# Second context attention: the order of three evacuations, and the context padded to 128 rows

## The reference

```
qh = (LN(x) @ Wq + bq)    16 heads of 8 channels
kh = ctx @ Wk + bk        77 x 128, from ctx of 77 x 64
vh = ctx @ Wv + bv
attn = softmax(qh kh^T / sqrt(8)) over the 77 context rows
x = x + concat(attn vh) @ Wo + bo
```

## Time and profile before

| | before |
|---|---|
| median of 3 runs | 4045.31 us |
| the profiled execution | 4050.56 us |
| its span | 4048.8 us |
| PE / PEld busy | 3845.5 us (95%) / 3012.5 us (74%) |
| DVE / ACT / POOL busy | 2922.8 (72%) / 2792.6 (69%) / 1902.7 us (47%) |
| granted TensorE clock, mean | 0.983 |
| the sublayer of the change | 3278.6 to 3689.2 us of the span |

### The profile page before, as it was taken

The page is one execution under the profiler, slowest core; times in us unless marked ns, Lnnn a source line. Parts: engine busy times, 40 slices in busy tenths (PEclk is TensorE's granted clock), DMA queues, the critical chain, the costliest instruction groups (busy, mean ns, idle before and its releaser), DMA issues. The chain is left out here.

```text
span 4048.8 us, 109312 instructions
## 1 busy us (share of the span) xinstructions
PE 3845.5 (95%) x35786; PEld 3012.5 (74%) x35786; DVE 2922.8 (72%) x7397; ACT 2792.6 (69%) x6292; POOL 1902.7 (47%) x1726
## 2 busy tenths in 40 slices
PE   8999899999989999898999989999999989998999
PEld 6777687888756666675666677888888867776777
DVE  7888655555479999658999955776777767775665
ACT  5555455555579999747999965777777767774333
POOL 5555322222278888526777753333333321112444
PEclk9999899999989999999999999999999989999999
DMA  1000100000100000100000010000000000000000
GB/s 30 19 19 19 52 7 6 6 6 6 41 9 8 8 8 8 29 16 9 8 8 8 12 29 30 1 0 0 0 0 0 0 3 3 3 3 6 12 12 13
DMA packets 118477, 46.71 MB, mean 12 GB/s; under 512 B 92256, under 2 KB 117088, under 8 KB 117728
## 3 DMA queue, kind: packets, MB, share of 16 engines
q1 hardware_dynamic: 118368, 45.30, 4.3%
HBM read 24.36 MB, written 4.19 MB: 7 GB/s over the span
## 5 line engine op out<-in xcount | busy, mean ns | idle before, releaser
L1102 POOL TENSOR_TENSOR l_rc<-l_rc,l_rs 128x1024 f32<-128x1024 f32 x128 | 303.7, 2373 | 202.3 <-DVE l_rs L1294 193.0
L1169 ACT ACTIVATE l_prob<-l_prob,l_mx 128x128 f32<-128x128 f32 x1024 | 312.9, 393 | 0.0
L670 POOL TENSOR_TENSOR ca_prob<-ca_prob,ca_sm 128x1232 f32<-128x1232 f32 x64 | 144.0, 2250 | 299.3 <-DVE ca_sm L836 299.3
L1780 POOL TENSOR_TENSOR mb_steps<-w_upto,mb_dta 128x1024 f32<-128x1024 f32 x64 | 121.5, 1898 | 345.7 <-DVE mb_dta L2048 345.7
L1194 PE MATMUL l_qk_ps<-w_local,l_hT 128*128 128x512 f32 x512 | 249.1, 610 | 13.0 <-DVE l_rs L1294 11.2
L1096 POOL TENSOR_TENSOR l_prob<-l_prob,l_sm 128x1024 f32<-128x1024 f32 x128 | 243.0, 1898 | 20.5 <-DVE l_sm L1280 20.5
L1079 POOL TENSOR_TENSOR l_rc<-l_rc,l_ss 128x1024 f32<-128x1024 f32 x128 | 243.6, 1903 | 12.5 <-POOL l_rc L1102 4.5
L1939 PE MATMUL mb_x_ps<-w_wx,mb_xT 128*128 128x256 f32 x1024 | 237.2, 385 | 0.0
L382 ACT ACTIVATE la_ef<-la_feat,la_fbias 128x1024 f32<-128x1024 f32 x128 | 135.7, 1111 | 121.8 <-PE la_feat L441 121.8
L2507 POOL TENSOR_TENSOR mo_hid<-mo_hid,mo_gate 128x1024 f32<-128x1024 f32 x64 | 121.8, 1903 | 201.3 <-DVE mo_hid L2653 201.3
L346 POOL TENSOR_SCALAR la_ef<-la_ef,la_high,la_low 128x1024 f32<-128x1024 f32 x128 | 151.4, 1193 | 134.6 <-ACT la_ef L382 134.6
(11 more groups left out here) (349 smaller groups left out, 11860.7 us busy)
## 6 DMA issues: line engine op xcount, KB each, us to landing
la_xin<-in_x SPq DMA_DIRECT2D x64, 64.0 KB
la_xT<-in_x_T SPq DMA_DIRECT2D x64, 64.0 KB, 1.8
l_h<-lt_y SPq DMA_DIRECT2D x128, 32.0 KB
lt_quad<-lt_y SPq DMA_DIRECT2D x32, 128.0 KB
out_x<-k_x SPq DMA_DIRECT2D x64, 64.0 KB, 1.5
l_h<-lt_y SPq DMA_DIRECT2D x128, 31.8 KB
lt_quad<-lt_y SPq DMA_DIRECT2D x32, 127.0 KB
ca_ctxT<-in_ctx_T SPq DMA_DIRECT2D x128, 19.2 KB
```

The source lines that it names most:

```text
L1102: gp.tensor_tensor(wide(rc[l][:]), wide(rc[l][:]), wide(rs[l][:]), ALU.add).then_inc(*pool_sum.did("rot"))
L1169: ex = sc.activation(p[:, a, j], p[:, a, j], ACT.Exp, bias=mx[l][:, a, j:j + 1])
```

## The change

On VectorE the value evacuation moves behind the reciprocal and the product. On ScalarE the keys are evacuated ahead of the queries; the waits that meant "both done" now name the queries, and the scores on TensorE wait for the queries too. `ctxT` gets 128 rows, of which the lower 64 are cleared once; `wk` and `wv` are taken with all 128 rows, so that the key and value products run over 128 rows. At the start GpSimd clears the small buffers and `ctxT` first and `vpad` last; the other engines no longer wait for `vpad`, only the value evacuation of the unrolled steps does. The transfers of the context wait for the clearing of `ctxT` once.

```diff
--- before.py
+++ after.py
@@ -2126,13 +2126,13 @@
     with ExitStack() as stack:
         m = Memory(nc, stack, "xa")
         part = g.context_part
-        wq, wk, wv, wo = part["wq"], part["wk"][0:CD], part["wv"][0:CD], part["wo"]
+        wq, wk, wv, wo = part["wq"], part["wk"], part["wv"], part["wo"]
         bq, bk, bv, bo = part["bq"], part["bk"], part["bv"], part["bo"]
         hmask, gmask = m.sb("hmask", [C, H]), m.sb("gmask", [C, 4])
         eps = m.sb("eps", [128, 1])
         stats, mv, rstd = both(m, "stats", [T, 6]), both(m, "mv", [T, 2]), both(m, "rstd", [T, 2])
         xn, xnT, qT = both(m, "xn", [T, C]), both(m, "xnT", [C, T]), both(m, "qT", [C, T])
-        ctxT, kT = both(m, "ctxT", [CD, S]), both(m, "kT", [C, S])
+        ctxT, kT = both(m, "ctxT", [128, S]), both(m, "kT", [C, S])
         kblock = both(m, "kblock", [C, 4, S])
         vpad = [m.sb(f"vpad{i}", [128, H // 2, 2 * WIDE]) for i in range(4)]
         prob = [m.sb(f"prob{i}", [T, H, S]) for i in range(4)]
@@ -2145,6 +2145,7 @@
         qkv_ps = m.ps("qkv_ps", [128, 512])
         out_ps = m.ps("out_ps", [128, 512])
         zeroed, prep, scaled, made = (m.sem(n) for n in ("zeroed", "prep", "scaled", "made"))
+        padded, cleared = m.sem("padded"), m.sem("cleared")
         c_in = m.lanes("c_in")
 
         vec_norm = Stage(m.sem("vec_norm"), "stats mv xn")
@@ -2153,7 +2154,7 @@
         vec_out = Stage(m.sem("vec_out"), "rden att attT x")
         act_norm = Stage(m.sem("act_norm"), "lnv rstd")
         act_turn = Stage(m.sem("act_turn"), "xnT")
-        act_key = Stage(m.sem("act_key"), "qT kT")
+        act_key = Stage(m.sem("act_key"), "kT qT")
         act_soft = Stage(m.sem("act_soft"), "exp")
         act_prob = Stage(m.sem("act_prob"), "pT0 pT1")
         act_out = Stage(m.sem("act_out"), "oT")
@@ -2164,7 +2165,7 @@
         pool_norm = Stage(m.sem("pool_norm"), "xb")
         pool_key = Stage(m.sem("pool_key"), "kb")
         NORM, TURN, KEY, SOFT, PROB, OUT = 0, 1, 2, 3, 5, 6
-        NZERO = 6
+        NZERO, NCLEAR = 2, 8
         by_head = lambda ap: ap.rearrange("p j (k e) -> p j k e", k=2)
         one = lambda b: flat(g.x[:, bass.ds(b.index, 1), :])
 
@@ -2177,24 +2178,28 @@
                         index = b.index if b.trip is None else sp.snap(b.index)
                         src = d["ctx_T"][bass.ds(index, 1)].rearrange("b c s -> (b c) s")
                         sp.wait_ge(*pe_key.at("qkv", b, ago=2))
-                        sp.dma_start(ctxT[b.lane][:], src).then_inc(c_in[b.lane], 16)
-
+                        sp.dma_start(ctxT[b.lane][0:CD], src).then_inc(c_in[b.lane], 16)
+
+                sp.wait_ge(padded, 2)
                 pipeline(sp, g.NB, OUT + 2, step, turn=4)
 
             @block.gpsimd
             def _(gp):
-                for i in range(4):
-                    gp.memset(vpad[i][:], 0.0).then_inc(zeroed, 1)
                 gp.memset(eps[:], LN_EPS).then_inc(zeroed, 1)
                 gp.memset(hmask[:], 1.0).then_inc(zeroed, 1)
+                for l in (0, 1):
+                    gp.memset(ctxT[l][:], 0.0).then_inc(padded, 1)
                 gp.wait_ge(zeroed, NZERO)
-                for i in range(4):
-                    gp.memset(by_head(vpad[i][:])[:, :, :, HD:HD + 1], 1.0).then_inc(zeroed, 1)
                 gp.affine_select(out=hmask[:], in_=hmask[:], compare_op=ALU.is_ge, fill=0.0, base=0,
                                  pattern=[[-HD, H]], channel_multiplier=1).then_inc(prep, 1)
                 gp.wait_ge(prep, 1)
                 gp.affine_select(out=hmask[:], in_=hmask[:], compare_op=ALU.is_ge, fill=0.0, base=HD - 1,
                                  pattern=[[HD, H]], channel_multiplier=-1).then_inc(prep, 1)
+                for i in range(4):
+                    gp.memset(vpad[i][:], 0.0).then_inc(cleared, 1)
+                gp.wait_ge(cleared, 4)
+                for i in range(4):
+                    gp.memset(by_head(vpad[i][:])[:, :, :, HD:HD + 1], 1.0).then_inc(cleared, 1)
                 pool_norm.start(gp)
                 pool_key.start(gp)
                 gp.wait_ge(g.fetched, g.NLAST)
@@ -2220,7 +2225,7 @@
                 sc.preload_act_table_set("natural_log_exp_and_others")
                 for stage in (act_norm, act_turn, act_key, act_soft, act_prob, act_out):
                     stage.start(sc)
-                sc.wait_ge(zeroed, NZERO + 4)
+                sc.wait_ge(zeroed, NZERO)
                 sc.wait_ge(g.fetched, g.NLAST)
                 sc.activation(bq, bq, ACT.Copy, scale=SCALE).then_inc(scaled, 1)
                 sc.wait_ge(scaled, 1)
@@ -2244,10 +2249,10 @@
                     if b:
                         l = b.lane
                         sc.wait_ge(*pe_key.at("qkv", b))
+                        sc.activation(kT[l][:], qkv_ps[:, T:T + S], ACT.Identity, bias=bk[:, 0:1]
+                                      ).then_inc(*act_key.did("kT"))
                         sc.activation(qT[l][:], qkv_ps[:, 0:T], ACT.Identity, bias=bq[:, 0:1], scale=SCALE
                                       ).then_inc(*act_key.did("qT"))
-                        sc.activation(kT[l][:], qkv_ps[:, T:T + S], ACT.Identity, bias=bk[:, 0:1]
-                                      ).then_inc(*act_key.did("kT"))
                     b = at(NORM)
                     if b:
                         l = b.lane
@@ -2273,7 +2278,7 @@
             def _(te):
                 for stage in (pe_turn, pe_key, pe_prob, pe_out):
                     stage.start(te)
-                te.wait_ge(zeroed, NZERO + 4)
+                te.wait_ge(padded, 2)
                 te.wait_ge(g.fetched, g.NLAST)
 
                 def heads(b, u):
@@ -2305,7 +2310,7 @@
                         l = b.lane
                         te.wait_ge(c_in[l], b.loaded())
                         te.wait_ge(*act_turn.at("xnT", b))
-                        te.wait_ge(*act_key.at("kT", b, ago=1))
+                        te.wait_ge(*act_key.at("qT", b, ago=1))
                         te.wait_ge(*vec_key.at("v", b, ago=1))
                         if at(OUT + 1):
                             te.wait_ge(*vec_out.at("x", at(OUT + 1)))
@@ -2333,6 +2338,7 @@
                     if b:
                         l = b.lane
                         te.wait_ge(*pool_key.at("kb", b))
+                        te.wait_ge(*act_key.at("qT", b))
                         if at(SOFT):
                             te.wait_ge(*vec_soft.at("sub", at(SOFT)))
                         for i in range(GROUPS):
@@ -2360,7 +2366,7 @@
                 for stage in (vec_norm, vec_key, vec_soft, vec_out):
                     stage.start(v)
                 v.wait_ge(g.fetched, g.NLAST)
-                v.wait_ge(zeroed, NZERO + 4)
+                v.wait_ge(zeroed, NZERO)
                 v.wait_ge(prep, 2)
                 v.tensor_reduce(gmask[:], hmask[:].rearrange("p (i h) -> p h i", h=4), AX, ALU.add).then_inc(made, 1)
 
@@ -2394,13 +2400,6 @@
                         v.wait_ge(*vec_norm.at("stats", b))
                         v.memset(rstd[l][:, 1:2], 0.0)
                         v.bn_aggr(mv[l][:], stats[l][:]).then_inc(*vec_norm.did("mv"))
-                    b = at(KEY)
-                    if b:
-                        v.wait_ge(*pe_key.at("qkv", b))
-                        v.wait_ge(*act_key.at("kT", b))
-                        split = lambda ap: ap.rearrange("p (j k e) -> p j k e", k=2, e=HD)
-                        v.tensor_tensor(by_head(vpad[b.slot][0:S])[:, :, :, 0:HD], split(qkv_ps[0:S, 2 * T:2 * T + C]),
-                                        split(bv[0:S]), ALU.add).then_inc(*vec_key.did("v"))
                     b = at(OUT)
                     if b:
                         l = b.lane
@@ -2411,6 +2410,15 @@
                         v.tensor_tensor(att[l][:].rearrange("p (h e) -> p h e", e=HD), pvT[:, :, 0:HD],
                                         rden[l][:].unsqueeze(2).to_broadcast([T, H, HD]), ALU.mult
                                         ).then_inc(*vec_out.did("att"))
+                    b = at(KEY)
+                    if b:
+                        v.wait_ge(*pe_key.at("qkv", b))
+                        v.wait_ge(*act_key.at("qT", b))
+                        if b.trip is None:
+                            v.wait_ge(cleared, NCLEAR)
+                        split = lambda ap: ap.rearrange("p (j k e) -> p j k e", k=2, e=HD)
+                        v.tensor_tensor(by_head(vpad[b.slot][0:S])[:, :, :, 0:HD], split(qkv_ps[0:S, 2 * T:2 * T + C]),
+                                        split(bv[0:S]), ALU.add).then_inc(*vec_key.did("v"))
                     b = at(NORM)
                     if b:
                         l = b.lane
```

## The result

| | before | after |
|---|---|---|
| median, us (4 runs each) | 4044.87 | 4016.55 (4015.51 to 4017.19) |
| ratio, 95% interval | | 0.9931 [0.9918, 0.9943] |
| profiled execution, its span, us | 4050.56, 4048.8 | 4015.51, 4013.8 |
| the stage (its first write on GpSimd to the first of the next stage), us | 410.67 | 383.77 |
| mean step, maxima of n = 9 to 63, us | 6.04 | 5.65 |

28.3 us faster; 42.9 were forecast, and the 4016.55 lie 1.6 above the range. The two profiled executions differ by 35.1 us, but 6.6 of it lie ahead of the stage and 1.5 behind it, where nothing was changed; the stage itself, 26.9 us shorter, is what is explained here. The last 1.4 us between that and the medians isn't traced.

What follows compares the result with a forecast made beforehand. The step of 6.04 us was taken as set by a loop through scores, products, evacuations, reciprocal, product and L2331. 38.4 (60 steps) + 1.8 (first steps) + 2.7 (start) = 42.9 us off, forecast 4002.5, range 3995 to 4015.

Steps and rivals of the forecast that it cites:

- S to L2322 at S+4.00: From a step's scores (S) to the transposes L2322: 4.00 us, set by VectorE's subtraction, instead of 4.16.
- S': Start of the next step's scores on TensorE, forecast at S+5.4, where S is the start of this step's scores.
- 5.40: Forecast step from scores to scores in us: 4.00 + 1.14 + 0.26, against 6.04 before, 0.64 less.
- a way to be wrong: Sign of failure: ScalarE, busy 4.6 us a step, becomes waited for; its half 0 evacuation has 0.1 us to spare.
- TensorE's 3.91: Time behind the scores at which TensorE alone would let L2322 start; VectorE's 4.00 was taken as later.
- L2322 to L2331 1.14: From transposes L2322 to transpose L2331 with the product ahead of the values: 1.14 us instead of 1.62, a gain of 0.48.
- the rival that went by it: TensorE's visible idle time only: TensorE gives back at most 0.28 us per step, 4024; chance 0.11.
- Padding 0.77 instead of 1.02: Products and neighbours on TensorE with one row count: up to 0.25 us less per step, of which 0.16 gained.
- the slower rival: Full-row weight loads stop running ahead under matmuls: step 6.31, 0.27 us more, 4057.7; chance 0.04.
- order only: Rival: gaps at L2313 and L2322 are weight loads and stay; step 5.56, 0.48 us less, 4012.7; chance 0.17.
- Keys first earns nothing alone and protects 0.12: Keys before queries on ScalarE: kblock 0.20 us ahead of the scores; with queries first, scores 0.12 late.
- Start and first steps, 2.7 + 1.8 = 4.5: At the start, vpad cleared behind the mask saves 2.7 us; four early steps waiting for kblock save 0.45 each, 1.8.

Runs made afterwards that it cites:

- a_turnfirst: Changed kernel with xnT's evacuation ahead of the exponential on ScalarE: 4007.43 us, 0.9906 of the kernel before, step 5.50.
- a_pvt: Changed kernel with the result's two transposes put in out_ps instead of score_ps, no longer waiting for the subtraction: 4006.72 us, step 5.49.
- a_waitlast: Changed kernel with the last add's two waits swapped, the one for xnT last: 4013.77 us, 0.9924 of the kernel before, step 5.56.
- a_nopad: Changed kernel with the key and value products over 64 rows again: 4020.23 us, 0.9939 of the kernel before, step 5.69.
- pvt_waits: Changed kernel with the result's transposes in out_ps and the late wait last for the add, the scores and kblock: 4000.84 us, step 5.34.
- a_qfirst: Changed kernel with queries evacuated ahead of keys again, the scores still waiting for the queries: 4020.28 us, step 5.71.
- b_order: Kernel before with one edit, reciprocal and product ahead of the value evacuation: 4025.75 us, 0.9954, step 5.72.
- pvt_waits_clear: As pvt_waits, but GpSimd clears two of the four vpad buffers only after VectorE's first two xn: 3999.91 us, step 5.34.
- b_start: Kernel before with one edit, the clearing of vpad moved behind the mask at the start: 4041.05 us, 0.9992 [0.9983, 1.0001], step 6.04.

## Why the prediction was wrong, by its own steps

**The step that failed: S to L2322 at S+4.00, "VectorE is later ... what is late next is the maximum and subtraction".** Measured: 4.30 (3504.20 to 3508.50). The subtraction stands behind the last add on VectorE, and the add waits for `xnT`: both read the bank `qkv_ps`. In the kernel before that wait was covered; `xnT` ended at 3506.31 and the add came at 3506.77, set by the maximum. `xnT` starts 3.4 us behind the L2322 before it (3.39 before, 3.36 after), whatever the scores do. With the predicted times it ends at S'+2.25, and the maximum would let the add go at S'+2.23; with the 0.24 that the add needs behind its release that is 0.26 late, and 5.40 becomes 5.66, measured 5.64. I had asked what the subtraction waits for only as far as the maximum, and listed ScalarE as a way to be wrong at another of its instructions (half 0), not at `xnT`. a_turnfirst (5.50) and a_pvt (5.49), two different ways out of that loop, bear it out: from the scores to this instruction they take 4.00, VectorE's figure in the prediction, and 3.87, near TensorE's 3.91. Taking away the wait alone wasn't tried, as ScalarE and VectorE would then read one PSUM bank at once. (The Trainium skill, PSUM — Partial Sum Buffer, PSUM bank collisions raise a hardware error, counts two reads by different engines among such collisions; no run here shows one.)

**The 0.24 itself.** In the unrolled steps at the stage's end `xnT` ends at 3625.10 and the add starts at 3625.19, 0.09 later, and the step is 5.49:

```profile
3624.84 0.26 ACT L2273 ACTIVATE xa_xnT<-xa_qkv_ps 128x128 f32<-128x128 f32 x1
3625.19 0.29 DVE L2387 TENSOR_TENSOR k_x<-k_x,xa_qkv_ps 128x128 f32<-128x128 f32 x1
```

In the hardware loop 0.15 comes on top. There VectorE's queue (DVEq) has register work of its own behind the wait for `xnT` (L2385): for the wait for `xb` (L2386) and for the add's address (L2387). Columns: count, ns min/median/max, first and last start:

```profile
L2387 DVEq FUSED_REGOPS  x56: 65/69/81, 3308.9 to 3619.6; - x56
...
L2386 DVEq ALU_OP  x56: 40/40/45, 3308.8 to 3619.5; - x56
```

Together 0.11 of the 0.15. What stands behind the wait that is released last is on the path: a_waitlast moved the one for `xb` ahead and took 0.09 off. That is twice the 0.04 of its register work, and no run shows where the rest comes from.

**L2322 to L2331 1.14:** right, 1.12 (3502.86 to 3503.98), against 1.62 before. The visible wait of the earlier trace rows, 0.28, would have undersold it by 0.2; the rival that went by it gives 4024.

**Padding 0.77 instead of 1.02:** right in size, 0.75, and the price went with the changes of row count, not with the weight loads, which stayed as long (0.30 us for the two of the keys in after, 0.29 before). The full-row loads kept running ahead (L2317 to L2318 0.33 as in the earlier trace rows), so the slower rival is out. But of the 0.16 counted in the sum the changed kernel gets 0.04 (a_nopad), since its TensorE then waits for the subtraction. In pvt_waits, where it doesn't, the padding brings 0.22. The total of 4016.55 lies near "order only" (4012.7) for the wrong reason: order alone gives 4025.75, and the gaps did go.

**Keys first earns nothing alone and protects 0.12:** `kblock` ends at 3509.46, 0.38 ahead of the scores of the longer step. Taken back it costs 0.06 (a_qfirst), but with the scores' wait for the queries left in. In the sum of 5.40 it would have had 0.20, and this is the second step that failed, hidden behind the first: the scores need 0.24 behind `kblock`, and `kblock` starts 0.16 behind the keys in the loop of after, not the 0.08 taken from the earlier trace rows. So 5.40 wasn't to be had with the waits in that order: a_pvt and a_turnfirst stop at 5.49 and 5.50. The 0.24 isn't a property of the hardware loop alone. b_order has 0.05 there, with the waits for `kblock` and the subtraction; a_pvt, a_qfirst and a_nopad have 0.24, and their scores wait for the queries too. So the wait that keys first made necessary seems to take 0.19 of the margin, more than the 0.12 that the edit was to protect; that isn't shown, as the wait by itself wasn't tried.

**Start and first steps, 2.7 + 1.8 = 4.5:** 3.1 measured. Counted from the stage's start the first scores come at 7.35 us (3279.36) instead of 9.84 (3288.43), 2.5 earlier, and those of n = 5 at 23.65 instead of 26.77, 3.1 earlier. `gmask` came at 0.90, about as forecast. Two things make up the missing 1.4 us. The first `xn` took 1.05 longer, held as below. And 0.48 was lost where TensorE's clock rises from 1.2 to 2.4 GHz: between the scores of n = 4 and those of n = 5 in both kernels, but later within that interval in after. The interval, in after and then in before (columns as in the earlier trace rows), was granted 0.52 in the one and 0.72 in the other, and is 6.38 instead of 5.90 long:

```profile
3289.28:3295.66 6.38, 6.38 (x31) 5.04 (x32) 4.31 (x9) 3.77 (x9) 1.28 (x3) 0.52 0.04 6
```

```profile
3299.46:3305.36 5.90, 5.40 (x31) 3.99 (x31) 4.17 (x8) 3.25 (x8) 1.11 (x2) 0.72 0.02 4
```

**Sum.** The 60 steps from the scores of n = 5 to those of n = 65 take 338.16 us instead of 362.25: 24.1 less where 38.4 stood, short 14.3. The start is 1.4 short, and 0.3 is lost behind n = 65. So 24.1 + 3.1 - 0.3 = 26.9, the stage's 26.9. The three edits alone bring 19.0 + 12.7 + 3.3 = 35.0, together 28.3 (in the profiled stages 19.0 + 11.9 + 1.5 = 32.4 and 26.9): their gains overlap, since each alone was freed to a different next wait.

## What to carry to other kernels

When a stall goes, follow every wait of what is late next, those that share a buffer included, and ask in which loop each lies: a loop that doesn't contain the instruction that got faster keeps its length. Add release-to-start distances from the same kind of step and with the same waits, since a margin smaller than that is no margin: from `kblock` to the scores it was 0.05 with two waits, 0.24 with three and 0.15 with the last-released of the three put last, all in the hardware loop. A new wait on an instruction may have a price of its own. And put the wait that is released last at the end of an instruction's waits: three such moves and one bank brought 4016.55 to 4000.84.

## What the runs showed of the hardware that was not expected

VectorE's `xn`, from SBUF to SBUF, takes 0.33 us in the median and 1.39 where it starts in the middle of GpSimd's clearing of `vpad`. The start of after, of pvt_waits_clear, and of a_waitlast:

```profile
3272.71 2.77 POOL L2199 MEMSET xa_vpad<- 128x768 f32 x4
3272.91 0.18 DVE L2371 TENSOR_REDUCE xa_gmask<-xa_hmask 128x4 f32<-128x16 f32 x1 [1.75 <-POOL xa_hmask L2196]
...
3274.17 1.39 DVE L2427 TENSOR_SCALAR xa_xn<-k_x,xa_mv,xa_rstd 128x128 f32<-128x128 f32 x1 [0.66 <-ACT xa_rstd L2262]
```

```profile
3273.81 1.41 POOL L2201 MEMSET xa_vpad<- 128x768 f32 x2
...
3275.27 0.34 DVE L2427 TENSOR_SCALAR xa_xn<-k_x,xa_mv,xa_rstd 128x128 f32<-128x128 f32 x1 [0.66 <-ACT xa_rstd L2264]
```

```profile
3272.73 2.85 POOL L2199 MEMSET xa_vpad<- 128x768 f32 x4
...
3274.19 0.71 DVE L2427 TENSOR_SCALAR xa_xn<-k_x,xa_mv,xa_rstd 128x128 f32<-128x128 f32 x1 [0.66 <-ACT xa_rstd L2262]
```

`xn` at 3274.17 ends at 3275.56, just behind the clearing's 3275.48; `gmask` at 3272.91, beside the same clearing, isn't held. b_start shows it too (1.38). a_waitlast has the same instructions there, yet `xn` takes 0.71: it ends at 3274.90, just behind the end of the third of the four writes (3274.82), and the fourth lasts 0.81 instead of the 0.74 of the others. So `xn` is held by one write at a time and can get in between two of them; of the kept traces with this start only this one shows it. The Trainium skill (SBUF — State Buffer, SBUF: two separate sides) has it that VectorE in a two-port mode and GpSimd share a pair of ports as an exclusive lock for the whole instruction. The traces agree with the hold and with its length by whole instructions; which mode `xn` ran in, no run here shows.
